# Routed experts with four places for transposed rows, TensorE products without a reader between stages, and an earlier compare in the scans' check

## The chip, the cores and the metric

The kernel runs on one core of a Trainium2 chip. The metric is the device time of one execution in microseconds (us), as the median of several runs. The core has a matmul engine (PE in the profile; its weight loads have a row of their own, PEld), a vector engine (DVE), an activation engine (ACT), GpSimd (POOL), which here issues gathers, and SyncE (SP), which issues all other transfers. The engines meet by counting semaphores only.

## The reference

The input x has 2 sequences of 2048 tokens with 512 channels. Four layers follow one another, each added to x:

```python
x = x + cond_layer(x, cond)       # per channel: x times a gate worked out from cond
x = x + rnn(x)                    # h = tanh(x_t @ Wx + h @ Wh + b), from token to token
x = x + moe(x, cond)              # 2 shared experts, and the 2 best of 8 routed experts, per token
x = x + leaky(cond, x)            # g = sigmoid(h @ Wh.T + z_t @ Wz.T + b); h = tanh(h * (1 - alpha) + g * z_t)

def moe(x, t):
    shared = sum(silu(x @ w1[e].T) * (x @ w3[e].T) @ w2[e].T for e in (0, 1)) / 2
    s = sigmoid([x, t] @ W_router.T); best two by s + bias; gates = s_best / sum(s_best)
    routed = sum(gelu(x @ r1[e].T) @ r2[e].T * gate[e] for e in best two)
    return (shared + routed) / 4
```

## The kernel before

**Stages.** `build` runs five blocks one behind the other: the first scan (`rnn`), the shared experts for half of the tokens (`shared_part` 0, with the router in it), the routed experts (`routed_part`), the other half of the shared experts (`shared_part` 1, which also gathers what the routed experts wrote), and the second scan (`leaky`). A block ends with a barrier of all engines, so a stage starts when the last engine has come out of the one before.

**Scans.** A sequence is cut into 32 segments that are scanned side by side, 16 chunks of 4 steps. A warm round comes first, then one full round (`full_round`). At its last step (`is_end`) DVE takes the difference of the states at the segments' ends from those before (L572) and its largest value per partition (L573); PE turns that column into a row of `pm` (L353); DVE takes the row's largest (L655) and compares it with a tolerance (L656). The outcome, `running`, is read by every engine (`over_rounds`: each waits until `check` has reached 4 and loads the word), and with it each branches to another round or out of the block. DVE's last sum of a chunk (L588, x plus state) releases SP's store of that chunk (L198).

**Shared experts.** 64 items for each half. An item is 24 products of 512 columns into `p1` (L1062) and 12 into `p2` (L1077), in PE's order: first(n), then second(n - 1). Ahead of the first item ACT and DVE split the first weights and the first x into 16-bit parts (L1209, L1507; L1191, L1320). In part 0 PE waits ahead of it for `zeroed`, then for these splits. `px` is a bank of PSUM for the router's small products; `listed` tells that the list of tokens per expert (`token_of`) has been read out of it.

**Routed experts.** 71 tiles of 128 rows, each of one expert. For each tile t: POOL gathers 128 rows of both 16-bit parts into one of four places `rows` (L1722); SP transposes them by a DMA into `xt` (`turn_x`, L1731); PE makes 12 products of 512 columns into `pf` (`first`); ACT applies gelu (L1807) and casts (L1811), DVE makes the low part (L1825); SP transposes that result (`turn_h`, L1737) into `ht`; PE makes 12 products into `py` (`second`); ACT scales into `y` (L1801), SP stores it (L1741). PE's order is first(0), first(1), first(2), second(0), first(3), second(1), and so on. There are two places for `xt`. The transposes of tiles 0 and 1 are issued in the stage before. SP's list, in order, is

```python
for q in range(LEAD): load of 768 KB into stage[q][:, 0:TILE]      # L1744, two
for t in range(SLOT_TILES):
    turn_x(t + 2)      # waits for rows_in (the gather) and f_done >= t + 1
    turn_h(t)          # waits for hs_ready >= t + 1
    if t == 0: store_last(...)      # 1 MB, L1684
    if t >= 2: store(t - 2)
    if t == 2: load of 1 MB into xres     # L1757
```

SP does these one after the other, so a wait in one holds up all behind it. The gather of tile t waits until the transpose of tile t - 4 has landed.

## Time and profile before

| | us |
|---|---|
| median of 3 runs | 1998.11 |
| the runs | 1996.50, 1998.11, 1998.31 |
| the profiled execution, its own time | 1998.5 |
| its span, first to last instruction | 1996.6 |
| PE busy | 1954.5 (98%) |
| DVE, ACT, POOL busy | 1107.8, 804.3, 141.3 |
| mean granted clock of PE | 0.994 |

The profile page gives busy time, the chain that ended last and the costliest groups of instructions over the whole span. Each stage also shows in the timeline (instructions in order of time with the idle time before them and what ended it), in the table by windows (busy time of each engine, PE's granted clock and the DMA share in a stretch) and in the list of waits. A product's printed length in the timeline includes its way through the array: behind one another, products start closer together than they are long.

### The profile page before, as it was taken

Reading aid. Unit: us, or ns where it says so; the run is one execution under the profiler, and the core shown is the slowest. Engines: PE = TensorE matmul, PEld = TensorE weight load, DVE = VectorE, ACT = ScalarE, POOL = GpSimd, SP = SyncE. Lnnn points to the kernel's source line nnn. Section 1 sums busy time; section 2 is a strip of 40 time slices with the busy share of each in tenths; the row PEclk is TensorE's granted clock in tenths of the full one; section 3 lists DMA queues with packets and bytes.
Section 4 is the critical chain, followed back from the end, with each engine's and each line's share of the span. In section 5 each row is a group of like instructions: output and inputs, shape, how many; then the busy total and the mean of one; then the engine's idle time right before and its main releaser. Section 6 shows DMA issues by size and latency. Waiting matters only on the chain. (4 is left out here: it accounts for less than half of the span.)

```text
span 1996.6 us, 45523 instructions
## 1 busy us (share of the span) xinstructions
PE 1954.5 (98%) x18076; PEld 1180.6 (59%) x18076; DVE 1107.8 (55%) x2366; ACT 804.3 (40%) x1701; POOL 141.3 (7%) x144
## 2 busy tenths in 40 slices
PE   8999979999999999999999999999999999999997
PEld 6999944444444444444444444444455555999997
DVE  5666556544895654111111147555665664778887
ACT  4444445432121433343333345322332332566664
POOL 0000000000000000111111112111101110000000
PEclk9999989999999999999999999999999999999999
DMA  7033238654342533999999965433332352101111
GB/s 298 17 136 142 109 141 224 195 170 136 132 163 85 190 106 128 218 205 203 201 205 204 188 201 181 141 90 90 100 96 69 101 156 94 45 3 43 42 42 45
DMA packets 281903, 266.37 MB, mean 133 GB/s; under 512 B 225991, under 2 KB 233293, under 8 KB 275086
## 3 DMA queue, kind: packets, MB, share of 16 engines
q1 hardware_dynamic: 270942, 228.73, 39.9%
q0 software_dynamic: 10800, 35.40, 6.7%
q8 instruction: 113, 1.85, 0.4%
q14 instruction: 48, 0.39, 0.1%
HBM read 153.70 MB, written 56.36 MB: 105 GB/s over the span
## 5 line engine op out<-in xcount | busy, mean ns | idle before, releaser
L1062 PE MATMUL sh_p<-xh,arena 128*128 128x512 f16 x2048 | 611.2, 380 | 8.6 <-DVE xl L1320 6.3
L1062 PE MATMUL sh_p<-xl,arena 128*128 128x512 f16 x1024 | 389.1, 380 | 0.0
L1062 PEld LDWEIGHTS sh_p<-xh,arena 128*128 128x128 f16 x2048 | 200.6, 98 | 252.1 <-issue 10.4
L1077 PE MATMUL p<-sh_h_hi,arena 128*128 128x512 f16 x1024 | 304.6, 379 | 0.0
L1825 DVE SCALAR_TENSOR_TENSOR ro_hs<-ro_h,fac,ro_hs 128x512 f16<-128x512 f32 x71 | 53.4, 752 | 306.3 <-ACT ro_hs L1811 270.9
L1232 ACT CAST sh_h_hi<-sh_half_h 128x512 f16<-128x512 f32 x128 | 79.1, 618 | 349.4 <-DVE sh_half_h L1590 346.0
L1768 PE MATMUL ro_pf<-arena,xres 128*128 x852 | 198.7, 384 | 7.1 <-DMA xres<-xl 4.8
L1768 PE MATMUL ro_py<-arena,ro_ht 128*128 x852 | 195.3, 379 | 0.7 <-DMA ro_ht<-ro_hs 0.7
L1226 ACT ACTIVATE sh_sig<-sh_p,fac 128x512 f32<-128x512 f32 x128 | 87.8, 686 | 268.1 <-PE sh_p L1062 268.1
L1077 PE MATMUL p<-sh_h_lo,arena 128*128 128x512 f16 x512 | 194.0, 379 | 0.0
L1062 PEld LDWEIGHTS sh_p<-xl,arena 128*128 128x128 f16 x1024 | 100.5, 98 | 121.6 <-issue 1.4
L1587 DVE SCALAR_TENSOR_TENSOR sh_half_h<-sh_sig,sh_p 128x512 f32<-128x512 f32 x128 | 87.6, 685 | 146.0 <-ACT sh_sig L1226 145.9
L1077 PEld LDWEIGHTS p<-sh_h_hi,arena 128*128 128x128 f16 x1024 | 96.7, 98 | 109.7 <-issue 0.4
L1768 PEld LDWEIGHTS ro_pf<-arena,xres 128*128 128x128 f16 x852 | 84.2, 99 | 110.7 <-issue 13.1
L1590 DVE TENSOR_TENSOR sh_half_h<-sh_half_h,sh_p 128x512 f32<-128x512 f32 x128 | 88.0, 688 | 109.2 <-PE sh_p L1062 106.2
L1768 PEld LDWEIGHTS ro_py<-arena,ro_ht 128*128 128x128 f16 x852 | 83.3, 98 | 101.4 <-issue 1.2
L1594 DVE TENSOR_TENSOR sh_h_lo<-sh_half_h,sh_h_hi 128x512 f16<-128x512 f32 x128 | 88.6, 692 | 71.7 <-ACT sh_h_hi L1232 71.2
L283 PE MATMUL leaky_acc<-leaky_x_hi,leaky_wx_hi 128*128 128x256 f32 x368 | 112.0, 304 | 1.5 <-DVEq L536 0.4
L1807 ACT ACTIVATE ro_h<-ro_pf,fac 128x512 f32<-128x512 f32 x71 | 48.8, 687 | 146.4 <-PE ro_pf L1768 146.4
L283 PE MATMUL leaky_acc<-leaky_x_hi,leaky_wx_lo 128*128 128x256 f32 x368 | 103.7, 282 | 0.0
L283 PE MATMUL leaky_acc<-leaky_x_lo,leaky_wx_hi 128*128 128x256 f32 x368 | 103.5, 281 | 0.0
L283 PE MATMUL rnn_acc<-rnn_x_hi,rnn_wx_hi 128*128 128x256 f32 x336 | 98.7, 309 | 2.7 <-issue 2.6
(272 smaller groups left out, 3100.2 us busy)
## 6 DMA issues: line engine op xcount, KB each, us to landing
stage<-in_shared_w SPq DMA_DIRECT2D x29, 768.0 KB, 5.3
routed_rows<-xres SPq DMA_DIRECT2D x71, 256.0 KB
stage<-in_norms_r SPq DMA_DIRECT2D x16, 1024.0 KB, 4.9
stage<-in_routed_w SPq DMA_DIRECT2D x16, 1024.0 KB, 4.8
stage<-in_norms SPq DMA_DIRECT2D x14, 1024.0 KB, 5.1
arena<-x SPq DMA_DIRECT2D x12, 1024.0 KB, 5.8
rnn_xs<-in_x SPq DMA_DIRECT2D x8, 1024.0 KB, 18.8
x<-xres SPq DMA_DIRECT2D x16, 512.0 KB, 2.6
```

The source lines that it names most:

```text
L283: mm = nc.tensor.matmul(acc[p][:, m, :], w[:, k, cols], x[p][:, k, :], start=(not gate and m % 2 == 0 and k == 0 and x is x_hi and w is wx ...
L1062: mm = nc.tensor.matmul(p1[u % P1][:], arena[:, w:w + P], x[slot(gl)][:, :, k, :], start=(j == 0), stop=(j == 3 * KD - 1))
L1077: mm = nc.tensor.matmul(p2[m][:], arena[:, w:w + P], h[n % 2][:], start=(i == 0 and j == 0), stop=(i == HID - 1 and j == 2))
L1226: nc.scalar.activation(sig[n % 2][:], p1[2 * n % P1][:], ACT.Sigmoid, scale=fac[:, 0:1]).then_inc(sig_ready, 1)
L1232: nc.scalar.copy(h_hi[n % 2][:], full_h[n % 2][:]).then_inc(hh_ready, 1)
L1587: nc.vector.scalar_tensor_tensor(half_h[n % 2][:], sig[n % 2][:], 2.0 ** -41, p1[2 * n % P1][:], ALU.mult, ALU.mult).then_inc(p1_free, 1)
L1590: nc.vector.tensor_tensor(full_h[n % 2][:], half_h[n % 2][:], p1[(2 * n + 1) % P1][:], ALU.mult).then_inc(p1_free, 1)
L1594: nc.vector.tensor_tensor(h_lo[n % 2][:], full_h[n % 2][:], h_hi[n % 2][:], ALU.subtract).then_inc(h_ready, 1)
L1768: mm = nc.tensor.matmul(out, a[:, lhs + k * P:lhs + (k + 1) * P], experts[:, bass.ds(e, 1), w0 + w + k * D:w0 + w + (k + 1) * D].rearrange ...
L1807: nc.scalar.activation(h[t % 2], pf[t % 2][:], ACT.Gelu, scale=fac[:, 2:3]).then_inc(g_done, 1)
L1825: nc.vector.scalar_tensor_tensor(hs[t % 2][:, D:2 * D], h[t % 2], fac[:, 3:4], hs[t % 2][:, 0:D], ALU.mult, ALU.subtract).then_inc(hs_read ...
```

## The change

There are four edits.

1. First scan, end of the full round: PE gets seven products of 128x512 in front of its wait for the check's column and four behind the product L353. They write `pg[0]`, which nobody reads by then. Shared part 0 gets 20 products of 128x128 ahead of its wait for `zeroed`, and five of 128x512 at its end, behind a wait for `listed`; both write `px`.
2. Check, in both scans: DVE's wait for PE's row, the reduce (L655) and the compare (L656) move from the end of the round into the last step, ahead of the product with the decay (L581, second scan only), of the last sum (L588) and of the copy L653.
3. Routed experts: four places for `xt`; the two new ones are the last quarters of the two stage buffers, beside the part that the 768 KB loads fill.
4. SP issues turn_x(2) and turn_x(3) ahead of its loop, and in the loop turn_x(t + 4) in place of turn_x(t + 2), with the same value of f_done awaited. POOL's and PE's waits on `xt_in` go by four semaphores.

```diff
                     full_chunks(pe, r, chunk)
+                    if gate:
+                        idle_products(nc, pg[0][:], wr_hi[:, 0, 0:P], wr_hi[:, 1, :], 7)
                     pe.wait_ge(check, (r - 1) * CHECK_LINKS + 2)
                     nc.tensor.matmul(pm[0:1, 0:P], mx[:, 0:1], ident[:], start=True, stop=True).then_inc(check_row, 1)
+                    if gate:
+                        idle_products(nc, pg[0][:], wr_hi[:, 0, 0:P], wr_hi[:, 1, :], 4)
...
+                        if is_end(c, o) and j == CHUNK_STEPS - 1:
+                            dve.wait_ge(check_row, turn[0])
+                            tied(nc.vector.tensor_reduce(mx[0:1, 3:4], pm[0:1, 0:P], AX.X, ALU.max))
+                            tied(nc.vector.tensor_scalar(running[:], mx[0:1, 3:4], TOL, None, ALU.is_gt))
                         if leaky:
                             dve.wait_ge(hi_ready, (s + 2) * parts)
...
                     nc.vector.tensor_copy(e_prev[:], hist[1][:, :, CW - LANES:CW - BATCH])
-                    dve.wait_ge(check_row, r)
-                    tied(nc.vector.tensor_reduce(mx[0:1, 3:4], pm[0:1, 0:P], AX.X, ALU.max))
-                    tied(nc.vector.tensor_scalar(running[:], mx[0:1, 3:4], TOL, None, ALU.is_gt))
...
                 if first_part:
+                    idle_products(nc, px[:, 0:P], keep["ident16"][:], keep["ident16"][:], 20)
                     pe.wait_ge(zeroed, 1)
...
                 second(ITEMS - 1)
+                if first_part:
+                    pe.wait_ge(listed, 1)
+                    idle_products(nc, px[:], keep["ident16"][:], h_hi[0][:], 5)
...
+def idle_products(nc, out, w, x, count):
+
+    for _ in range(count):
+        nc.tensor.matmul(out, w, x, start=True, stop=True)
...
-    return [both[:, i * 2 * D:(i + 1) * 2 * D] for i in range(2)]
+    behind = [s[:, TILE:MATRIX].bitcast(F16) for s in keep["stage"]]
+    return [both[:, i * 2 * D:(i + 1) * 2 * D] for i in range(2)] + behind
...
-                    pool.wait_ge(xt_in[t % 2], 16 * ((t - RING) // 2 + 1))
+                    pool.wait_ge(xt_in[t % XT], 16 * ((t - RING) // XT + 1))
...
                     sp.wait_ge(rows_in[t % RING], 16 * (t // RING + 1))
-                    if t >= 2:
-                        sp.wait_ge(f_done, t - 1)
-                    sp.dma_start_transpose(xt[t % 2].rearrange("p (q n) -> p q n", n=P), rows[t % RING]).then_inc(xt_in[t % 2], 16)
+                    if t >= XT:
+                        sp.wait_ge(f_done, t - XT + 1)
+                    sp.dma_start_transpose(xt[t % XT].rearrange("p (q n) -> p q n", n=P), rows[t % RING]).then_inc(xt_in[t % XT], 16)
...
+                for t in range(2, XT):
+                    turn_x(t)
                 for t in range(SLOT_TILES):
-                    if t + 2 < SLOT_TILES:
-                        turn_x(t + 2)
+                    if t + XT < SLOT_TILES:
+                        turn_x(t + XT)
                     turn_h(t)
...
-                    pe.wait_ge(xt_in[t % 2], 16 * (t // 2 + 1))
+                    pe.wait_ge(xt_in[t % XT], 16 * (t // XT + 1))
                     if t >= 2:
                         pe.wait_ge(g_done, t - 1)
-                    product(pf[t % 2][:], xt[t % 2], e, 0).then_inc(f_done, 1)
+                    product(pf[t % 2][:], xt[t % XT], e, 0).then_inc(f_done, 1)
```

## Rows read from the trace of the kernel before

**Rows 1.** The page's first line.

```profile
span 1996.6 us, 45523 instructions
```

**Rows 2.** Timeline of PE, first scan to shared part 0: start us, length us, what.

```profile
262.93 0.65 PE L300 MATMUL rnn_acc<-rnn_h_lo,rnn_wr_hi 128*128 128x64 f16 x16
265.40 0.38 PE L353 MATMUL rnn_pm<-ident,rnn_mx 128*1 128x128 f32 x2 [1.83 <-DVE rnn_mx L573]
272.13 1.01 PE L1062 MATMUL sh_p<-xh,arena 128*128 128x512 f16 x2 [6.35 <-DVE xl L1320]
...
277.94 0.38 PE L1062 MATMUL sh_p<-xl,arena 128*128 128x512 f16 x1
```

**Rows 3.** Windows there: stretch, length, busy PE, PEld, DVE, ACT, POOL, clock, DMA.

```profile
267.50:268.00 0.50, 0.00 (x0) 0.00 (x0) 0.00 (x0) 0.00 (x0) 0.00 (x0) 0.59 0.99 393
```

**Rows 4.** Timelines of DVE and SP there, and one row of SP's waits (264 to 275).

```profile
266.25 0.27 DVE L655 TENSOR_REDUCE rnn_mx<-rnn_pm 1x1 f32<-1x128 f32 x1
266.56 0.14 DVE L656 TENSOR_SCALAR rnn_running<-rnn_mx 1x1 int32<-1x1 f32 x1
...
266.17 0.33 SPq L198 DMA_DIRECT2D x<-xres  x1
...
SPq L161 <- PEq L161: 1.6, 1, 1.6
```

**Rows 5.** Timeline of DVE and PE, shared part 0 to routed experts.

```profile
782.35 2.48 DVE L1308 SCALAR_TENSOR_TENSOR arena<-stage,scl,arena 128x1024 f16<-128x1024 f32 x2 [1.77 <-ACT arena L1186]
...
783.28 0.38 PE L1077 MATMUL p<-sh_h_lo,arena 128*128 128x512 f16 x1
786.02 7.04 PE L1768 MATMUL ro_pf<-arena,xres 128*128 x24 [2.36 <-PEq L895]
794.69 2.76 PE L1768 MATMUL ro_pf<-arena,xres 128*128 x12 [1.62 <-DMA xres<-xl]
797.28 2.75 PE L1768 MATMUL ro_py<-arena,ro_ht 128*128 x12
803.19 4.45 PE L1768 MATMUL ro_pf<-arena,xres 128*128 x12 [3.15 <-DMA xres<-xl]
807.48 2.75 PE L1768 MATMUL ro_py<-arena,ro_ht 128*128 x12
```

**Rows 6.** Windows of the routed experts: at the start, and from 808 us on.

```profile
786.00:786.50 0.50, 0.48 (x2) 0.29 (x3) 0.50 (x2) 0.40 (x1) 0.50 (x1) 0.91 1.59 184
...
808.00:1158.00 350.00, 350.00 (x1624) 158.62 (x1623) 54.11 (x72) 138.45 (x208) 59.07 (x62) 1.00 0.92 201
```

**Rows 7.** Timeline of SP's issues and of POOL's first gather there.

```profile
785.11 0.81 SPq L1744 DMA_DIRECT2D stage<-in_shared_w  x2
790.55 1.24 SPq L1731 DMA_TRANSPOSE xres<-xl  x1
792.76 1.23 SPq L1737 DMA_TRANSPOSE ro_ht<-ro_hs  x1
...
794.72 2.00 SPq L1731 DMA_TRANSPOSE xres<-xl  x1
796.77 2.47 SPq L1737 DMA_TRANSPOSE ro_ht<-ro_hs  x1
799.34 3.31 SPq L1731 DMA_TRANSPOSE xres<-xh  x1
...
785.75 0.94 POOL L1722 DMA_INDIRECT xh<-x_rows,token_of  x1 [125.78 <-POOLq L895]
```

**Rows 8.** DMAs that write or read xres, 780 to 840 us: issue to landing.

```profile
DMA to landing us min/median/max: 3.9/4.6/8.3
```

**Rows 9.** Timeline of DVE at the end of the second scan.

```profile
1990.05 0.49 DVE L578 TENSOR_TENSOR leaky_h_lo<-leaky_hist,stage 128x128 f16<-128x128 f32 x2
...
1990.80 0.42 DVE L588 TENSOR_TENSOR leaky_xo<-leaky_xs,leaky_hist 128x256 f32<-128x256 f32 x1
```

**Rows 10.** Windows behind the last compute: the last chunk's store.

```profile
1992.00:1993.00 1.00, 0.00 (x0) 0.00 (x0) 0.00 (x0) 0.00 (x0) 0.00 (x0) 0.50 0.94 385
```

5 lines of the change are left out of this document (3 added, 2 removed).

## The prediction

> **What bounds the kernel now.** I read the span first [rows 1] and PE's busy share in the table above it: 98%. So whatever the four edits can give back lies in the few microseconds in which PE stands still or runs at the lower clock. The timeline of PE around each barrier shows these, the windows show the granted clock, the timelines of SP and DVE show what comes last. In the middle of the routed stage there is nothing to win: from 808 to 1158 us PE is busy for all of 350 us at clock 1.00, with the DMA engines at 0.92 [rows 6].
>
> Every time below is in us of the profiled execution.
>
> *First scan to shared part 0.* The scan's last products end at 263.6, the check's product runs at 265.40, the first shared product at 272.13 [rows 2]. Between 267.5 and 268.0 the granted clock falls from 2.4 to 1.2 GHz (mean 0.59 in that half microsecond) [rows 3], some 4 us after the scan's last dense products. So the shared stage starts slow: from 272.13 to 277.94 it starts 14 products [rows 2], while at the full clock one takes 0.216 (2.59 for 12, the distance from 794.69 to 797.28 [rows 5]). 14 x 0.216 = 3.0, against 5.8: **2.8 us lost to the clock**.
>
> *Shared part 0 to routed.* PE ends at 783.6 and comes back at 786.02; DVE's last split ends at 784.83, so the barrier waits for DVE, not for PE [rows 5]. The clock falls inside 786.0 to 786.5 (mean 0.91) [rows 6], when PE is already back. The 24 products of tiles 0 and 1 take 7.04 as printed, less the 0.16 by which a printed group of twelve (2.75) outlasts its distance to the next (2.59): they hold PE until 792.9, where 24 x 0.216 = 5.2 would give 791.2, **1.7 lost**. Then PE waits for x of tile 2 until 794.69 (**1.8**), and from 799.9 for x of tile 3 until 803.19 (**3.3**); the clock falls again and first(3) takes 4.3 in place of 2.6 (**1.7**) [rows 5]. Together 8.5.
>
> *The end.* The last sum starts at 1990.80, and behind it only the last store and the way out follow: the store moves data in 1992 to 1993 [rows 9, 10], the span ends at 1996.6 [rows 1].
>
> **The change, part by part.**
>
> *Eleven products at the end of the first scan.* Seven take 7 x 0.216 = 1.5 and end near 264.9; the check's product waits for DVE until 265.40 anyway [rows 2], so they hide. They'd cost if they ran at the lower clock: 3.0, to 266.4, one late. The four behind it take 0.9, to about 266.7. PE's wait for the outcome is queued behind them, and the outcome came at 266.70 before [rows 4]. They cost nothing as long as it comes no earlier, and otherwise eat what the compare gives.
>
> *Twenty small products in shared part 0.* A quarter of the columns each: an estimate from 0.216 is 1.1 in all at the full clock and 2.1 at the lower. They start when the barrier opens, near 269.8 (SP's wait for PE there began 1.6 earlier, and PE was the last at it [rows 4]), and end at 270.9 or 271.9. PE isn't wanted before 272.13 [rows 2]; what hides them is the splitting of the first x. If that were 1 us shorter they would cost at the lower clock.
>
> *What the clock gives there.* No row shows a gap of this kind filled in part. Of the 8.5 us between 263.6 and 272.13, 3.5 or so get filled: two pauses remain, 3.1 (266.7 to 269.8) and 1.2. The lower bound is nothing: the 2.4 us pause before 786.02 sufficed to bring the clock down [rows 5, 6], and this one is longer. The upper bound is all 2.8, if the clock never falls. The 24 products at 786 got the clock back before they were done; at 272 it took 5.8 us of half-rate work. The nearest row for a partial gain is one of 1.7, what the shorter slow stretch at 786 lost. I take half of that, **-0.85**, as I can't tell whether it falls on the good side. The Trainium skill ("TensorE: Matmul & The Clock Gate", Part 1) says that the same kernel runs into the switch at different points in different runs. The runs of before lie 1.8 apart, which fits a switch of this size; by that rule the gain here would be 0 in some runs and 1.7 or 2.8 in others.
>
> *The compare moved up, first scan.* DVE's reduce and compare stood behind the last sum and the copy: 266.25 to 266.70 [rows 4]. Now they start when PE's row is there, near 265.9, and the outcome comes at about 266.3: up to 0.4 earlier for ACT and PE. The last sum starts 0.6 later, at 266.35, and so SP issues its store at 266.8 in place of 266.17; queued behind it are SP's own wait for the outcome and the barrier. SP had 1.6 of slack there, waiting for PE [rows 4], so this hides. Gain between 0 (the four products eat it) and 0.4: **-0.35** if PE's sequencer does not wait for its array; I take that.
>
> *The compare moved up, second scan.* Here nothing hides it. The two low parts end at 1990.54. Wait, reduce, compare (0.27 + 0.14 and the hops between them, as spaced in the first scan: 266.25 to 266.70) are 0.45 to 0.6 ahead of the product with the decay and the last sum. The last sum and with it the last store move from 1990.80 to about 1991.36: **+0.56**. What leaves from the other end (reduce and compare, to 1991.77) had lain beside the store's flight, so nothing is given back. Bounds 0.4 and 0.7 [rows 9, 10].
>
> *Five products at the end of shared part 0.* 1.1, from 783.5 to 784.6; `listed` had come long ago (the gathers of tiles 0 to 3 need it and are over), so the wait is free. DVE arrives at 784.83 [rows 5], so they hide. The pause shrinks from 2.4 to 1.3. If the clock holds, PE has tiles 0 and 1 done at 791.2.
>
> *Four places, and the order on SP.* The wait on f_done in the loop has the same value at the same turn, so the only new freedom at the start is that x of tiles 2 and 3 is issued right behind the two loads, near 786, and not at 790.55 and 794.72 [rows 7]. Before, x of tile 3 was queued behind the 1 MB store (L1684, between the issues at 792.76 and 794.72) and took 8.3 to land, where 4.1 (790.55 to 794.69) is what tile 2 took [rows 5, 7, 8]. But the DMA engines are at work on the loads' 1.5 MB until about 791 (1.57 MB at the 385 GB/s at which the last store of the program moves [rows 10] are 4.1 us, and I allow 1.8 from the issue at 785.11 [rows 7] to the first byte). I put x of tile 2 at 793.0 (bounds 790, 4.1 behind its new issue, and 794.7, as before), and x of tile 3 1.3 later.
>
> What is late next is h. On SP, turn_x(4) now stands ahead of turn_h(0). It waits for the gather of tile 4, issued at 785.75, which passes the same DMA engines as the loads [rows 7]; I put its landing at 792. Then turn_x(4) issues to 793.3, turn_h(0) to 794.5 (before: 792.76 to 793.99), and h(0) lands 4.1 behind its issue, at 797.5. Queued behind that: the 1 MB store, turn_x(5), turn_h(1), each as before with an x in front, 0.5 to 1 later than the 796.77 of before [rows 7]; one more gather shares the engines. With 7 to 8 us from its issue, as its neighbour x(3) had, h(1) lands at 804.5 to 805.6. PE's run is then: first(2) 793.0 to 795.6; second(0) 797.6 to 800.2; first(3), in place, to 802.8; second(1) from 805.1. Before, second(1) started at 807.48 [rows 5]: **-2.4**. From there h(2), behind turn_x(6), has 5 us of room, and so does h(3) behind the 1 MB load. So of 8.5 some 6 stay, as waits for h in place of waits for x. Bounds: 0.7, if the clock falls in the wait for h(1) and takes its 1.7 again, and 8.5.
>
> The Trainium skill ("DMA: Bandwidth & Descriptors", Anatomy of one DMA) says that the DMA engines never wait on a semaphore, the issuing sequencer does. That is the rule that speaks against this order: turn_h(0) can't pass a turn_x(4) that waits. The trace's spacing of SP's issues agrees.
>
> *Sum.* -0.85 - 0.35 - 2.4 + 0.56 = -3.0. The profiled execution took 1998.5 (span 1996.6 and 1.9 around it), 0.4 above the median. 1998.5 - 3.0 = 1995.5, and against the median 1998.1 - 3.0 = **1995.1**.
>
> **The rivals.**
>
> *A. The x transposes were the whole trouble.* h(0) and h(1) land in time, because the loads leave room and x no longer queues behind the store; both clock losses of the routed start go. For it: x of tile 3 alone lost 3.3 and 1.7 [rows 5]. Against: SP's order. Routed start -4.5 to -8.5, first boundary -1.7 to -2.8, compare +0.2: between -6 and -11, likeliest -6.1: 1992.0. The whole of it is 1987.0.
>
> *B. The queue ahead of h decides (slower).* Behind 1.5 MB of loads each transpose may take not 1.24 but 3.31 to issue, as the one at 799.34 did [rows 7]. Then x(2), x(3), x(4) are out at 785.9 + 9.9 = 795.8, h(0) at 799.1, the store takes 0.6, and x(5) and h(1) are out at 803.0 and 806.3, and with 8.3 from h(1)'s issue start at 803.0 to landing [rows 8] second(1) starts at 811.3, 3.8 later than before; one more fall of the clock makes it 5.5. With +0.56 - 0.35: 2002.1 to 2003.8. It decides from the point where turn_h(1) is issued more than 2.5 us later than at 796.77. Against: x(2) at 790.55 was issued in 1.24 while the loads were still moving.
>
> *C. The products and places do nothing that shows.* The clock falls as before (pauses of 3.1 and 1.3 are left) and h(1) comes when x(3) used to and PE waits as long: -0.7 in the routed stage, +0.2 in the checks: 1997.6.
>
> **How the numbers follow.** My forecast 0.50, with its own range 1993.4 (both clock terms whole) to 1996.9; A 0.25; C 0.18; B 0.07. A change of 0.2%, 4.0 us, is about the least that a measurement tells from none. Faster by more than that means below 1994.1: A nearly whole (0.23) and a third of the forecast's lower side (0.15): 0.38. Slower, above 2002.1: most of B, 0.05. The rest, 0.57, lies within. For 8 in 10 the range goes from 1990.5, which takes in most of A, to 1998.3, which takes in C.
>
> **What would show it.** In the trace after: the first shared product's clock and the distance of its first 14 products; the two windows at 267.5 and at 272 to 278; PE's first product of the routed stage some 1 to 3 earlier, its 24 products in 5.2; who releases first(2), second(0), first(3) and second(1): h in place of x if I'm right, none if A is; SP's turn_h(0) and turn_h(1) against 792.76 and 796.77; the last sum of the second scan 0.56 later behind its step's low parts. Wrong would make me: a gather of tile 4 that lands before 790, which puts turn_h(0) in front; loads whose share of the DMA engines delays x(2) beyond 795; or new code that shifts the way of an engine through the branch and the barriers, of which no row of before gives a price.

## The result, and the profile after

| | before | after |
|---|---|---|
| median, us | 1998.32 (10 runs, 1996.02 to 2000.51) | 2003.07 (10 runs, 2001.64 to 2011.41) |
| ratio to before, with its 95% interval | | 1.0033 (1.0025 to 1.0041) |
| the profiled execution, us | 1998.5 | 2001.64 |
| its span | 1996.6 | 1999.8 |
| PE busy | 1954.5 | 1957.7 |

The change makes the kernel slower by 4.8 us. I had forecast 3.0 us less. The profiled execution of after is the shortest of its ten, so the trace shows 3.2 us of the 4.8.

Where they lie: I go from boundary to boundary. The first line of the routed experts starts at the same time in both traces, so everything ahead of it evens out.

PE from the end of the first scan to shared part 0, timeline of the kernel after (start, length, what, idle before and who ended it):

```profile
263.82 1.67 PE L1684 MATMUL rnn_pg<-rnn_wr_hi 128*128 128x512 f16 x7
265.80 0.38 PE L355 MATMUL rnn_pm<-ident,rnn_mx 128*1 128x128 f32 x2 [0.32 <-DVE rnn_mx L577]
266.12 1.04 PE L1684 MATMUL rnn_pg<-rnn_wr_hi 128*128 128x512 f16 x4
271.61 2.24 PE L1684 MATMUL sh_px<-ident 128*128 128x128 f16 x20 [4.46 <-PEq L161]
273.91 1.01 PE L1067 MATMUL sh_p<-xh,arena 128*128 128x512 f16 x2
```

The windows of after in the same stretch (stretch, length, busy time of PE, PEld, DVE, ACT, POOL, granted clock, DMA share, GB/s):

```profile
267.50:268.00 0.50, 0.00 (x0) 0.00 (x0) 0.00 (x0) 0.00 (x0) 0.00 (x0) 1.00 0.02 8
271.00:272.00 1.00, 0.39 (x5) 0.42 (x6) 0.00 (x0) 0.41 (x1) 0.00 (x0) 0.86 0.11 25
272.00:273.00 1.00, 1.00 (x12) 1.00 (x10) 0.65 (x1) 1.00 (x3) 0.20 (x1) 0.50 0.63 70
275.00:276.00 1.00, 1.00 (x5) 0.39 (x4) 1.00 (x3) 1.00 (x3) 0.00 (x0) 0.94 1.00 410
```

At 267.5, where before fell to the lower level [rows 3], the clock of after is still at 2.4 GHz. It falls at the end of 271 and is back early in 275, so only the small products and the first few real ones run slow. But PE comes out of the barrier at 271.6 and meets its first real product at 273.91, 1.8 later than before [rows 2]. The clock's gain and this delay cancel: the 24 products of the routed experts start at 786.01, before at 786.02 [rows 5].

PE at the start of the routed experts, timeline of after:

```profile
783.50 1.24 PE L1684 MATMUL sh_px<-sh_h_hi,ident 128*128 128x512 f16 x5
786.01 5.35 PE L1788 MATMUL ro_pf<-arena,xres 128*128 x24 [1.27 <-PEq L900]
797.54 4.34 PE L1788 MATMUL ro_pf<-arena,stage 128*128 x12 [6.18 <-DMA stage<-xl]
802.07 2.76 PE L1788 MATMUL ro_py<-arena,ro_ht 128*128 x12 [0.18 <-DMA ro_ht<-ro_hs]
...
809.04 2.76 PE L1788 MATMUL ro_py<-arena,ro_ht 128*128 x12 [1.62 <-DMA ro_ht<-ro_hs]
...
820.79 2.76 PE L1788 MATMUL ro_py<-arena,ro_ht 128*128 x12 [1.22 <-DMA ro_ht<-ro_hs]
```

Here is the loss. PE is done with tiles 0 and 1 at 791.2, 1.7 earlier than before, and then waits 6.18 for x of tile 2, where before it waited 1.62 [rows 5]. first(2) starts 2.85 later, at 797.54, at the lower clock; second(1) starts at 809.04 against 807.48, and one more wait, for h of tile 3, follows at 820.79. In sum the trace of after is even with before at 786, 1.6 behind at second(1), 3.3 behind at the start of shared part 1 (1168.15 against 1164.81) and 3.2 behind at the end.

SP's issues in that stretch, timeline of after:

```profile
785.12 0.81 SPq L1762 DMA_DIRECT2D stage<-in_shared_w  x2
785.98 7.67 SPq L1749 DMA_TRANSPOSE stage<-xl  x2
796.00 1.23 SPq L1749 DMA_TRANSPOSE xres<-xh  x1
797.27 1.33 SPq L1755 DMA_TRANSPOSE ro_ht<-ro_hs  x1
...
802.50 3.13 SPq L1755 DMA_TRANSPOSE ro_ht<-ro_hs  x1
```

x of tile 2 is issued at 785.98 in place of 790.55 [rows 7], 4.6 earlier, and lands later: 11.6 from issue to first(2), where before took 4.1. The two transposes take SP 7.67 to issue. Then SP stands still until 796.00, because turn_x(4) waits for the gather of tile 4 (f_done, its other wait, was up since about 789), and turn_h(0) is behind it, 4.5 later than before.

What the DMA engines did, windows of before and then of after:

```profile
791.00:793.00 2.00, 2.00 (x10) 0.74 (x8) 0.75 (x1) 0.92 (x2) 0.00 (x0) 1.00 1.27 241
795.00:797.00 2.00, 2.00 (x11) 0.89 (x10) 0.33 (x1) 0.00 (x0) 1.15 (x1) 1.00 1.08 380
```

```profile
789.00:791.00 2.00, 2.00 (x11) 0.88 (x9) 0.71 (x1) 1.22 (x2) 0.00 (x0) 1.00 1.00 351
791.00:793.00 2.00, 0.36 (x2) 0.00 (x0) 0.16 (x2) 1.41 (x2) 0.00 (x0) 1.00 1.26 104
793.00:795.00 2.00, 0.00 (x0) 0.00 (x0) 0.63 (x1) 0.00 (x0) 0.00 (x0) 0.74 0.91 199
795.00:797.00 2.00, 0.00 (x0) 0.00 (x0) 0.00 (x0) 0.00 (x0) 0.00 (x0) 0.50 1.35 132
```

Up to 791 the loads stream as before. From 791 to 797 the DMA engines of after are busy (share 1.26, 0.91, 1.35) and move only 104 to 199 GB/s; before moved 241, 170 and 380 in the same three windows. What PE waits for isn't idle, it is slow. The queues' rows tell whose packets were slow. Queue q0 has the gathers, q1 all that SP issued. From 790 to 792, packets, MB and share of the 16 engines' time of q0, before and then after:

```profile
q0 software_dynamic: 144, 0.49, 61.2%
q0 software_dynamic: 37, 0.14, 94.5%
```

In before 144 packets of the two gathers start in these 2 us, and x of tile 2 is issued only at 790.55. In after, where its transpose is already queued, 37 start, and they take more of the engines' time than the 144 did. From 792 to 794 only 16 are left in before, which then has 991 packets in q1; after still has 41 in q0 and 176 in q1.

The end of the second scan, timeline of after:

```profile
1992.61 0.49 DVE L582 TENSOR_TENSOR leaky_h_lo<-leaky_hist,stage 128x128 f16<-128x128 f32 x2
...
1994.09 0.42 DVE L596 TENSOR_TENSOR leaky_xo<-leaky_xs,leaky_hist 128x256 f32<-128x256 f32 x1
```

From the low parts to the last sum it is 1.48, before 0.75 [rows 9]: 0.73 more.

### The profile page after: what moved, and what is told of

Its sections match the earlier page's. It is cut to its first block and busy times, and to the rows that moved or that the text cites. A ratio compares the mean times of both kernels' runs of the same rounds, so it can differ in the third digit from the quotient of the medians.

```text
span 1999.8 us, 45594 instructions
## 1 busy us (share of the span) xinstructions
PE 1957.7 (98%) x18112; PEld 1183.3 (59%) x18112; DVE 1108.1 (55%) x2366; ACT 804.6 (40%) x1701; POOL 141.8 (7%) x144
## 5 line engine op out<-in xcount | busy, mean ns | idle before, releaser
L1788 PE MATMUL ro_pf<-arena,stage 128*128 x420 | 97.9, 384 | 6.2 <-DMA stage<-xl 6.2
L1788 PE MATMUL ro_pf<-arena,xres 128*128 x432 | 99.0, 379 | 1.3 <-PEq L900 1.3
```

What stands on the lines that cost most here:

```text
L1788: mm = nc.tensor.matmul(out, a[:, lhs + k * P:lhs + (k + 1) * P], experts[:, bass.ds(e, 1), w0 + w + k * D:w0 + w + (k + 1) * D].rearrange ...
```

## The experiments

Sixteen kernels ran, each in several rounds beside the kernel before; the ratio is to the runs of before on the same chip. The last three columns are from each kernel's one trace: the time from PE's first routed product to first(2), to second(1), and to the first product of shared part 1 (the whole stage). They can be compared across kernels whatever happened ahead of the routed stage.

| kernel | median, us | before | ratio (95%) | to first(2) | to second(1) | whole stage |
|---|---|---|---|---|---|---|
| before | | | | 8.7 | 21.5 | 378.8 |
| after | 2003.07 | 1998.32 | 1.0033 (1.0025, 1.0041) | 11.5 | 23.0 | 382.1 |
| e1 edits 3 and 4 | 2004.76 | 1998.27 | 1.0041 (1.0026, 1.0056) | 11.5 | 24.6 | 382.6 |
| e2 edit 1 | 1996.54 | 1998.27 | 0.9992 (0.9983, 1.0000) | 8.7 | 18.2 | 376.2 |
| e3 edit 2 | 1998.87 | 1998.27 | 1.0004 (0.9995, 1.0012) | 8.7 | 21.2 | 378.5 |
| e4 e1, loads late | 1999.63 | 1998.27 | 1.0008 (0.9999, 1.0017) | 5.2 | 18.6 | 378.7 |
| e5 four places, SP's old list | 2001.52 | 1997.83 | 1.0018 (1.0009, 1.0027) | 11.5 | 21.7 | 383.1 |
| e6 e1, h ahead of x | 2006.28 | 1997.83 | 1.0045 (1.0031, 1.0059) | 11.1 | 23.9 | 386.0 |
| e7 before, loads late | 1999.61 | 1997.83 | 1.0006 (0.9997, 1.0015) | 6.4 | 17.6 | 375.6 |
| e8 the five products | 1998.33 | 1997.83 | 1.0005 (0.9996, 1.0014) | 8.3 | 18.8 | 376.2 |
| e9 e1, transposes ahead of the loads | 2001.60 | 1998.15 | 1.0022 (1.0013, 1.0031) | 5.2 | 22.3 | 380.1 |
| e10 e1, gathers held | 2003.44 | 1998.15 | 1.0026 (1.0016, 1.0036) | 7.1 | 24.7 | 382.4 |
| e11 before, 1 MB store and load late | 1996.52 | 1998.15 | 0.9994 (0.9985, 1.0003) | 8.5 | 18.0 | 377.3 |
| e12 e11 with edit 1 | 1997.92 | 1998.15 | 1.0003 (0.9994, 1.0012) | 8.8 | 18.3 | 377.5 |
| e13 e1, gathers early | 1999.94 | 1998.14 | 1.0009 (1.0000, 1.0018) | 7.2 | 21.2 | 378.9 |
| e14 before, gathers early | 1998.56 | 1998.14 | 0.9997 (0.9988, 1.0005) | 7.0 | 20.0 | 377.3 |
| e15 two places, edit 1, gathers early, 1 MB store and load late | 1995.15 | 1998.14 | 0.9982 (0.9973, 0.9990) | 7.7 | 17.1 | 376.2 |
| e16 as e15 with edits 3 and 4, 768 KB loads at the end | 1994.22 | 1998.14 | 0.9983 (0.9972, 0.9993) | 5.2 | 17.1 | 375.5 |

The time to first(2) repeats well: 8.3 to 8.8 in the six kernels in which x of tile 2 waits for first(0) and follows the loads (before, e2, e3, e8, e11, e12), 11.1 to 11.5 in the four (after, e1, e5, e6) in which it is issued right behind the loads with the gathers under way. The four kernels with the routed code of before fall in two pairs: before and e3, whose first 24 products ran partly at the lower clock, have 21.5 and 21.2 to second(1) and 378.8 and 378.5 for the stage, e2 and e8, whose 24 ran at 2.4 GHz, 18.2 and 18.8, and 376.2 both. So these columns are read only beside the medians. Five traces are of executions well below their kernel's median, by 3.3 to 4.4 us (e4, e6, e7, e9, e13); what the longer executions of these kernels lost, and where, no trace shows.

The explanations in play after the result were four: SP's order (h behind an x that waits), the loads ahead of the transposes, the gathers beside them, and the products that delay the way through the first barrier. The expectations give them letters; each says what its letters stand for.

**Which edit.** First each edit alone.

e1, the places and SP's list alone (edits 3 and 4 of the diff, whole functions `turned_x` and `routed_part`, and the four `xt_in`).

> The kernel before with edits 3 and 4 alone: four places for xt, and SP's list with turn_x(2) and turn_x(3) ahead of its loop and turn_x(t + 4) in it. Theory Q (the queue): in the changed kernel the two transposes behind the 1.5 MB of loads took 7.67 us to issue, x of tile 2 let PE wait until 797.54, and turn_h(0) came 4.5 us later than before; PE reached second(3) 2.95 us later although its clock had held. Alone, with the clock lost at the start as before, this gives 3 to 6 us over the kernel before, and most of the 4.8 that the changed kernel is over it in the medians. Rival P (the products and the longer way out of the first scan cost the time): alone, these two edits are within 1.5 us of the kernel before.

6.5 us slower than before, a little beyond the 3 to 6 of theory Q and far from rival P. Its trace repeats that of after (24 products in 5.35, 6.12 of waiting for x of tile 2, turn_h(0) at 798.15), 1.1 later, without any of the idle products.

e2, the idle products alone (edit 1).

> The kernel before with edit 1 alone, all 36 products without a reader. Theory Q: they give back clock: 1.7 us at the start of the routed stage, up to 2.6 at the start of shared part 0, against up to 1.5 for a later barrier (the changed kernel's PE came out of the first scan's branch 4.9 us behind the compare, before 3.1): the time is 1 to 3 us under the kernel before. Rival P: the products hold PE up on its way through the branch and the barrier and cost more than the clock gives: 1 to 4 us over.

1.7 faster, interval 0 to 3.4.

e3, the compare alone (edit 2).

> The kernel before with edit 2 alone, the compare ahead of the last sums in both scans. Theory Q: +0.7 us in the second scan (the trace of the changed kernel has 3.29 of distance from the low parts to the end where before it was 2.57 at the step before), 0 to -0.4 in the first: +0.3 to +0.7, not to be told from none. Rival: the later store of the first scan holds the barrier: +1.0 or more.

0.6 slower, not told apart from none; the 0.73 of the trace of after lies in the interval. The three medians add up to 6.5 - 1.7 + 0.6 = +5.4, where all together measured +4.8. The loss is in the routed edits.

**SP's order.** e6 is e1 with the loop turned round:

```diff
-                    if t + XT < SLOT_TILES:
-                        turn_x(t + XT)
                     turn_h(t)
+                    if t + XT < SLOT_TILES:
+                        turn_x(t + XT)
```

> Edits 3 and 4 alone, with turn_h(t) ahead of turn_x(t + 4) in SP's loop. Theory L in its first form (turn_x(4) holds turn_h(0) up until the gather of tile 4 has come): h(0) is issued near 791 in place of 797, PE waits for it no more, 2 to 4 us under the 6.5 that the list with x ahead costs: 2000 to 2002. Rival M (the two transposes behind the loads are the cost): h(0) is queued behind their 7.5 us of issuing all the same, x of tile 2 lands near 797: within 1.5 us of the kernel with edits 3 and 4.

SP and PE in e6, timeline:

```profile
784.32 7.23 SPq L1734 DMA_TRANSPOSE stage<-xl  x2
791.59 3.38 SPq L1740 DMA_TRANSPOSE ro_ht<-ro_hs  x1
...
795.42 5.30 PE L1773 MATMUL ro_pf<-arena,stage 128*128 x12 [5.71 <-DMA stage<-xl]
```

turn_h(0) gets out 7.2 behind PE's first product, in e1 11.0 (798.15 against 787.12), and nothing is won: 8.5 slower than before. PE still waits 5.7 for x of tile 2. That turn_x(4) stands ahead of turn_h(0) is not the cause.

e5 keeps SP's list of before, with four places (the diff is against e1):

```diff
-                for t in range(2, XT):
-                    turn_x(t)
                 for t in range(SLOT_TILES):
-                    if t + XT < SLOT_TILES:
-                        turn_x(t + XT)
+                    if t + 2 < SLOT_TILES:
+                        turn_x(t + 2)
```

> Four places for xt, but SP's list as before: no transpose ahead of the loop, turn_x(t + 2) in it. Only x of tile 2 comes earlier (it no longer waits for f_done), right behind the loads; x of tile 3 stays behind h(0) and the 1 MB store. The kernel with edits 3 and 4 alone was 6.5 us over the kernel before. Theory L (the list, two x in a row and x(t + 4) ahead of h(t)): this kernel loses most of that, 0 to 2.5 us over the kernel before. Rival M (any transpose behind the 1.5 MB of loads, beside the gathers, is slow): x of tile 2 lands near 797 and PE waits for it as long: 4 us over or more.

The difference to before is that every turn_x waits for two tiles less: turn_x(2) not for first(0), turn_x(5) for first(1) and not for first(3), and so on. The trace of e5:

```profile
785.92 0.81 SPq L1747 DMA_DIRECT2D stage<-in_shared_w  x2
786.78 2.29 SPq L1734 DMA_TRANSPOSE stage<-xl  x1
...
798.28 5.20 PE L1771 MATMUL ro_pf<-arena,stage 128*128 x12 [6.12 <-DMA stage<-xl]
...
808.09 0.40 SPq L1760 DMA_DIRECT2D xres<-x  x1
808.59 1.42 SPq L1734 DMA_TRANSPOSE xres<-xh  x1
...
817.98 2.76 PE L1771 MATMUL ro_pf<-arena,xres 128*128 x12 [1.56 <-DMA xres<-xh]
```

Against PE's first product x of tile 2 is issued 4.5 earlier than before (786.78 with 786.80, before 790.55 with 786.02), and it comes 11.5 after that issue, not 4.1. The kernel loses 3.7, more than theory L allowed and a little less than rival M. But that one transpose isn't where its trace loses them. x of tile 3 is there by then, so first(3) runs without the wait of 3.15 that before has, and second(1) starts 21.7 behind PE's first product, before 21.5. The stage's other 4.1 come later, most of them in two more waits for x: 1.56 for tile 5 at 817.98 and 1.92 for tile 7 at 830.43. Tile 5 shows the same thing once more. Before held turn_x(5) back until first(3) was done, 3.0 us behind the 1 MB load (807.72 against 804.72), and it landed 5.3 later (813.06); e5 issues it 0.5 behind that load, and it lands 9.4 later.

**The loads.** e4 is e1 with the two 768 KB loads at turns 12 and 14:

```diff
-                for q in range(LEAD):
-                    sp.dma_start(keep["stage"][q][:, 0:TILE], src["shared_w"][q + 1]).then_inc(stage_in, 16)
...
                     turn_h(t)
+                    if t in (12, 14):
+                        q = (t - 12) // 2
+                        sp.dma_start(keep["stage"][q][:, 0:TILE], src["shared_w"][q + 1]).then_inc(stage_in, 16)
```

> Edits 3 and 4 alone, and SP's two loads of 768 KB moved from the start of the routed stage to the turns of tiles 12 and 14, where nothing waits for them soon. Theory Q: with no loads in front, the two early transposes issue in 1.24 us each and land some 4 us later, near 790; PE has x of tile 2 in time, h(0) lands by 795, and the routed stage begins 5 us or more faster than in the kernel before: 1990 to 1995. Rival H (SP's order is what costs, turn_x(4) waiting for the gather in front of turn_h(0)): the gathers still come when they come, and the gain against the kernel before is under 2 us.

Timeline of e4, SP, POOL and PE:

```profile
783.16 2.61 SPq L1734 DMA_TRANSPOSE stage<-xl  x2
787.25 0.94 POOL L1725 DMA_INDIRECT xl<-x_rows,token_of  x1 [1.27 <-DMA stage<-xl]
...
795.21 4.04 PE L1774 MATMUL ro_py<-arena,ro_ht 128*128 x12 [3.23 <-DMA ro_ht<-ro_hs]
```

POOL's gather of tile 6 starts when x of tile 2 has landed: 787.25, 4.1 behind its issue. Two transposes are issued in 2.61, not in 7.24 as in e1. PE runs through tile 2 without a stop and then waits for h(0). Of the 6.5 us, 5.1 come back. Theory Q had put the kernel at 1990 to 1995, below before, and that was missed: by its median e4 is no faster than before, as rival H had it, since waits for h take the place of those for x (3.23 here, 2.03 at 815.24).

e7 is the same move in the kernel before.

> The kernel before with one thing changed: SP's two loads of 768 KB are issued at the turns of tiles 12 and 14, not at the start of the routed stage. It tells what the loads themselves cost. If the loads are what x of tile 2 and the gathers wait for, PE's 1.8 us wait for x(2) and part of the 3.3 for x(3) go: 2 to 5 us under the kernel before. If the order of x, h and the store decides, x(2), issued when f_done is 1, lands as before and the time is within 1 us.

1.8 slower, no clear difference, and neither of the two outcomes expected. In its trace first(2) comes 2.3 earlier, PE still waits 3.25 for x of tile 3, behind the 1 MB store, and the whole stage is 3.2 shorter than before's; but this execution lies 4.0 below the kernel's median, and what the others lose no trace shows. In the medians, then, late loads give nothing to the kernel before and 5.1 to the one with early transposes: the gain of e4 is not a plain gain of loads out of the way.

e9 is e1 with the two transposes ahead of the two loads.

```diff
+                for t in range(2, XT):
+                    turn_x(t)
                 for q in range(LEAD):
                     sp.dma_start(keep["stage"][q][:, 0:TILE], src["shared_w"][q + 1]).then_inc(stage_in, 16)
-                for t in range(2, XT):
-                    turn_x(t)
```

> Edits 3 and 4 alone (6.5 us over the kernel before), with the two early transposes issued ahead of the two loads and not behind them. Theory M (transposes behind loads in flight are what is slow: 11.5 us from issue to landing in two traces, 4.1 without the loads): x of tiles 2 and 3 land some 4 us behind their issue, PE has no wait for x, and the kernel is 3 us or more under the one with edits 3 and 4, though waits for h stay: -2 to +3 against the kernel before. Rival G (it is the gathers of tiles 4 and 5, in flight at the same time, that the transposes hinder and wait for): no better than 1.5 us under the 6.5.

Timeline of e9:

```profile
783.70 2.61 SPq L1734 DMA_TRANSPOSE stage<-xl  x2
786.36 1.48 SPq L1749 DMA_DIRECT2D stage<-in_shared_w  x2
788.44 4.12 SPq L1734 DMA_TRANSPOSE xres<-xh  x1
792.61 4.39 SPq L1740 DMA_TRANSPOSE ro_ht<-ro_hs  x1
...
799.14 5.19 PE L1773 MATMUL ro_py<-arena,ro_ht 128*128 x12 [6.62 <-DMA ro_ht<-ro_hs]
```

first(2) runs at once, and the wait has moved on to the transposes that now stand behind the loads: x(4) takes 4.12 to issue, h(0) 4.39, and PE waits 6.62 for h(0). Three of the 6.5 come back. Whatever transpose follows the loads pays. The Trainium skill ("DMA: Bandwidth & Descriptors", Queues, rings and completion order) says that each DMA engine takes the descriptors of one ring in their order; e1 and e9, which differ in that order alone, agree with it (11.5 behind the loads, 4.1 ahead of them). The two new places in the stage buffers aren't slow in themselves: x of tile 2 goes to the same place in e1 and in e9.

**The gathers.** In e10 POOL issues the gathers of tiles 4 and 5 only when x of tile 3 has landed:

```diff
+                pool.wait_ge(xt_in[3], 16)
                 for t in range(RING, SLOT_TILES):
```

> Edits 3 and 4 alone, and POOL holds its first gathers of the routed stage (tiles 4 and 5) until x of tile 3 has landed, so that loads and the two early transposes have the DMA engines to themselves. Rival G: the transposes land by 794, as soon as the 1.5 MB are through (4.1 us), in place of 797.5. Theory M: they take as long, near 797. In either case the gathers, and with them turn_x(4) and turn_h(0) behind it, come later, so the time may be over the 6.5 us; the landing of x of tile 2, read from when PE starts first(2), is what tells.

Timeline of e10:

```profile
787.84 5.85 SPq L1735 DMA_TRANSPOSE stage<-xl  x2
...
794.95 2.76 PE L1774 MATMUL ro_pf<-arena,stage 128*128 x12
805.18 4.26 PE L1774 MATMUL ro_py<-arena,ro_ht 128*128 x12 [7.47 <-DMA ro_ht<-ro_hs]
```

The loads are ahead as in e1, but x of tile 2 is there within 7.1 of its issue. That is between the two forecasts, nearer to rival G's. So the loads alone go with some 3 of the 7.4 above 4.1, and the rest needs the gathers beside them. The kernel doesn't gain (+5.3), since the held gather now holds turn_x(4) and h(0) behind it.

e13 takes the gathers out of the way without holding anything: POOL issues them in the stage before, once the transposes of tiles 0 and 1 have landed.

```diff
+                    for t in range(ROWS_RING, ROWS_RING + 2):
+                        pool.wait_ge(keep["xt_in"][t - ROWS_RING], 16)
+                        nc.gpsimd.indirect_dma_start(row_ring(keep, t), None, dram["xt"], bass.IndirectOffsetOnAxis(ap=token_of[:, t:t + 1], axis=0)
+                                                     ).then_inc(keep["rows_in"][t % ROWS_RING], 16)
...
-                for t in range(RING, SLOT_TILES):
+                for t in range(RING + 2, SLOT_TILES):
```

> Edits 3 and 4 alone, with POOL's gathers of tiles 4 and 5 issued at the end of shared part 0, as soon as the transposes of tiles 0 and 1 have landed, and not at the start of the routed stage. Theory G (loads, transposes and gathers in flight together are what is slow): x of tiles 2 and 3 land within 3 us of the loads' end, turn_x(4) waits for no gather, turn_h(0) is issued by 794, and the time is 0 to 3 us over the kernel before in place of 6.5. Rival M (transposes behind loads alone are slow): first(2) starts 11 us behind the issue as before, 5 us over or more.

Timeline of e13:

```profile
784.88 5.84 SPq L1738 DMA_TRANSPOSE stage<-xl  x2
...
792.12 1.34 SPq L1744 DMA_TRANSPOSE ro_ht<-ro_hs  x1
...
792.08 2.76 PE L1777 MATMUL ro_pf<-arena,stage 128*128 x12 [1.83 <-DMA stage<-xl]
```

7.2 from issue to first(2) again, turn_x(4) right behind the others (at 790.83), h(0) at 792.12. 1.8 slower than before: 4.7 of the 6.5 us are back, with the loads where they were, as theory G had it. e14, the same move in the kernel before, does nothing:

> The kernel before with the same two gathers issued in the stage before. Theory G: x(2), issued at 790.55 into the gathers' data, lands a little sooner; x(3), behind the 1 MB store, does not: 0 to 2 us under the kernel before. Rival M: no difference, within 0.5.

+0.4 in the medians, and PE's two waits for x are 1.62 and 3.36, much as before. So in the medians the early gathers are worth something only where the transposes are early.

Set side by side, from the SP and PE timelines of each trace, where PE waited for x of tile 2 (in e10 it was there by first(2) at the latest):

| | x(2) issued after the loads' issue | issue to use | loads' issue to use |
|---|---|---|---|
| gathers under way: after, e1, e5, e6 | 0.9 | 11.1 to 11.6 | 12.0 to 12.4 |
| gathers under way: e2, e8, e11, e12 | 3.7 | 5.9, 5.5, 5.7, 6.0 | 9.6, 9.2, 9.4, 9.7 |
| gathers under way: before, e3 | 5.4, 5.3 | 4.1, 4.3 | 9.6, 9.6 |
| gathers elsewhere: e10, e13 | 0.9 | 7.1, 7.2 | 8.0, 8.1 |
| gathers elsewhere: e14, e15 | 3.7 | 4.1, 4.8 | 7.9, 8.6 |

With the transposes ahead of the loads or the loads away it is 4.1 (e4, e9) or 3.5 (e7) from issue to landing with the gathers under way and 5.1 without (e16). Read down the last column: behind the loads, x of tile 2 comes 7.9 to 8.6 after their issue, whenever it was issued itself, as long as no gather is beside them. With the gathers it comes at 9.2 to 9.7 if it is issued 3.7 or more behind the loads, and at 12.0 to 12.4 if it is issued at once. In these rows an earlier issue wins nothing, and beside the gathers the earliest one loses some 3.

**The products.** e8 has only the five products at the end of shared part 0.

> The kernel before with only the five products at the end of shared part 0. All 36 products together gave 1.7 us. If the clock at the start of the routed stage is what they give back, this alone gives it: PE's first 24 products in 5.3 and not 7.0, but x of tile 2 lands when it did, so the 1.7 turn into a longer wait for x and the time stays within 0.5 us. The other theory, that the gain reaches the end: 1 to 1.7 us under.

Timeline of e8, SP and PE:

```profile
788.26 0.81 SPq L1753 DMA_DIRECT2D stage<-in_shared_w  x2
791.98 1.24 SPq L1740 DMA_TRANSPOSE xres<-xl  x1
...
789.14 5.35 PE L1777 MATMUL ro_pf<-arena,xres 128*128 x24 [1.25 <-PEq L895]
797.48 4.03 PE L1777 MATMUL ro_pf<-arena,xres 128*128 x12 [2.99 <-DMA xres<-xl]
```

The 24 products are fast, and up to first(2) what they gain becomes a longer wait for x: 2.99, where before it was 1.62. The table above has the reason: x is issued 1.7 earlier behind the loads (3.7, not 5.4) and comes hardly earlier (9.2, not 9.6). Behind it the trace does better than before: the wait for x of tile 3 is 0.84 and not 3.15, and the whole stage is 2.6 shorter. The medians still show no gain (+0.5, interval from 0.8 faster to 2.8 slower). The two fit together if the executions of before mostly have a stage as short as e8's and its trace shows one of the longer, which a single trace can't show. And the 5.35 isn't the products' doing alone: of the twelve kernels without these five, nine have it too (e1, e4, e5, e6, e7, e9, e11, e13, e14), and three have 6.90 to 7.04 (before, e3, e10). All six with them have 5.35.

**Store and load of 1 MB.** e11 is before with store_last at turn 4 in place of 0 and the 1 MB load at turn 6 in place of 2, e12 the same with edit 1.

```diff
-                    if t == 0:
+                    if t == 4:
                         store_last(sp, keep, 0, x_out)
...
-                    if t == 2:
+                    if t == 6:
```

> The kernel before with the 1 MB store issued at the turn of tile 4 and the 1 MB load at the turn of tile 6, in place of 0 and 2. x of tile 3 was queued behind that store and took 8.3 us to land, and PE waited 3.3 us for it and lost 1.7 to the clock behind the wait. Theory L2 (the store in front of x(3) is the cost): x(3) lands 4 to 5 us behind its issue, before PE wants it, and the time is 3 to 5 us under the kernel before. Rival: the waits move to tiles 5 to 7, within 1 us.

1.6 faster, interval from 3.0 faster to 0.6 slower, less than the 3 to 5 of theory L2. The wait for x of tile 3 is gone (turn_x(3) is issued at 793.83 in 1.26), that for x of tile 2 is not (3.19).

> The kernel before with edit 1 (all products) and the store and load of e11. If both gains are real and independent, -1.7 and -3 to -5: 4 to 7 us under the kernel before. If the store's place gives nothing: -1.7.

No difference. The two gains, -1.7 and -1.6, neither of them clear of none by itself, didn't add here; beside e11, edit 1 gave nothing.

**Together.** e15 joins what did no harm in the kernel with two places; e16 adds the four places, with the 768 KB loads at turns 66 and 67.

> Two places for xt as before, with all products of edit 1, the 1 MB store and load at tiles 4 and 6, and the two gathers in the stage before. Single gains measured: 1.7 for the products, 1.6 for the store's place, neither beyond its interval. If they add up with the gathers': 3 to 5 us under the kernel before. If each only fills the gap that another leaves, as the products with the late store did (0.2 under): 0 to 2.

3.0 faster than before (0.9982, 0.9973 to 0.9990).

> Edits 1, 3 and 4 with everything that collided taken apart: the two gathers in the stage before, the two 768 KB loads at the turns of tiles 66 and 67, the 1 MB store and load at tiles 4 and 6. Theory G: PE has no wait at the start of the routed stage beyond 1 us and its clock holds: 6 to 9 us under the kernel before, 1989 to 1992. Rival T (four places let SP and POOL run transposes and gathers ahead of h, in a stage whose DMA engines are 0.92 busy, whatever the start looks like): waits for h stay, and it is no more than 3 us under.

3.9 faster by the medians, 0.9983 (0.9972 to 0.9993) by the ratio, where theory G had hoped for 6 to 9. PE of e16, timeline:

```profile
785.99 5.35 PE L1791 MATMUL ro_pf<-arena,xres 128*128 x24 [1.26 <-PEq L899]
791.18 2.75 PE L1791 MATMUL ro_pf<-arena,stage 128*128 x12
796.25 4.45 PE L1791 MATMUL ro_py<-arena,ro_ht 128*128 x12 [2.32 <-DMA ro_ht<-ro_hs]
```

One wait is left at the start, for h as rival T had it, and the clock falls in it. Both kernels beat before and after, and they aren't told from one another. e16 differs from e15 in the four places and in the late 768 KB loads together, so what these runs show is that the pair brings nothing measurable over two places; four places alone, with the gathers early and the loads where they were, weren't tried against e15.

## Why the prediction was wrong

**The step that failed: "I put x of tile 2 at 793.0 (bounds 790, 4.1 behind its new issue, and 794.7, as before)".** It came at 797.5. The upper bound rested on the thought that an earlier issue can't land later. It can: in before, the wait for first(0) held the transpose back until the loads were nearly through, the gathers' packets went ahead of its own, and it then took 4.1; issued right behind the loads, with the gathers beside it, it takes 11.1 to 11.6. I had priced that wait as a cost, and it was one that did good. The first half of the sum was right, though no row had the 1.8 that I allowed from the loads' issue to their first byte: in the trace bytes move by 786.1, some 1.0 behind it, the loads stream until 791, and the two land 6.6 behind their issue, near 792. I then added the 2 us that were left of a transpose in free air, where the trace shows six more at 104 to 199 GB/s. By the trace of after, first(2) came 4.5 later than forecast and second(1) 3.9 later, so that the term of -2.4 measured +1.6. Another 1.8 is lost between second(1) and the end of the stage, where I had put nothing: I gave h(3), behind the 1 MB load, 5 us of room, and PE waits 1.22 for it at 820.79. It was issued at 812.63 and took 8.2 to its use. By the medians four places with the new list cost 6.5 (e1), four places with the old one 3.7 (e5).

**"What is late next is h": right, and too small.** turn_x(4) did wait for the gather of tile 4, with turn_h(0) behind it. I put that gather's landing at 792; turn_x(4) was issued at 796.00. h(0) was to land at 797.5 and was used at 802.07, h(1) at 809.04 in place of 804.5 to 805.6. But that order isn't what costs: with h in front (e6) the time is no better. The rule that I had weighed against the change (a sequencer's wait holds up what is behind it) is seen in SP's standing still from 793.65 to 796.00, and it wasn't the one that decided.

**Rival B had the mechanism.** Transposes behind 1.5 MB of loads were to take 3.31 each to issue, and from turn_h(1) more than 2.5 us late on it was to decide; the first two took 7.67 and turn_h(1) came 5.7 late (802.50 against 796.77). Its total was 2002.1 to 2003.8, and the median is 2003.07. I gave it 0.07, on the ground that x(2) "was issued in 1.24 while the loads were still moving". At 790.55 they were nearly through: the row showed the end of the queue, not its middle. The rows at 796.77 to 799.34 (2.47, 3.31) [rows 7], issued behind 1 MB in flight, were the nearer ones. B's path to the loss was not exact either: it had PE late from h(1) on, with second(1) 3.8 to 5.5 later than before, and the trace shows it late from x(2) on and second(1) 1.6 later. That its total fits the median is in part luck. Nor did B name the gathers, without which 4.7 of the 6.5 come back (e13).

**The clock at the first boundary: -0.85, of the right size as far as the traces tell.** The mean granted clock from 262 to 286 us is 0.93, 0.86, 0.86, 0.93 and 0.93 in the five kernels with edit 1 (after, e2, e12, e15, e16), and 0.79 in eight, 0.86 in five of the thirteen without the products of the scan. From the first shared product to the first routed one PE takes 511.7 to 512.9 in those five and 512.4 to 513.9 in the thirteen, 0.7 less in the mean, and the trace of before has the 513.9: so its 2.8 lost to the clock is likely more than most executions lose. In whole times the gain isn't shown. e2 is 1.7 faster, with an interval that reaches 0, and e12, which is e11 with edit 1, is 1.4 slower than e11, within their intervals. The Trainium skill ("TensorE: Matmul & The Clock Gate", Part 1), by which the same work meets the switch at different points in different runs, agrees with these rows, and with the 24 products at 786, which took 5.35 or 7 in kernels that are alike up to there.

**The 1.7 lost at 786 was partly an accident of one trace.** I read 7.04 [rows 5] as what the kernel does. Nine of twelve kernels without the five products show 5.35. So for most executions there may have been little for the five products to give back, and no gain from them is measured (e8, +0.5).

**The barrier.** PE came out of the first one at 271.6, 1.8 later than before, though the compare ended at the same time (266.67 and 266.70). I had named this as a way to be wrong ("new code that shifts the way of an engine through the branch and the barriers"). The products aren't needed for it: ACT's wait for the barrier is 4.7 in before and 6.0 in after, but of the twelve other kernels whose scan has no added product seven have 6.3 to 6.8 (e1, e3, e5, e7, e8, e10, e14) and five 4.0 to 4.3 (e4, e6, e9, e11, e13). It varies by up to 2.8 us between traces of the same code, and the trace of before was one of the short ones. All five with the products have 6.0 to 6.6, which so few traces can't tell from chance. So the 786.01 against 786.02 is a coincidence of two traces. The twenty small products cost nothing, but only just: they end at 273.85, and the first part of x is split at about 273.9 (DVE's split starts at 273.02, and 0.90 lay between its start and PE's product in before).

**The compare: -0.35 and +0.56.** In the first scan the new place saves 0.44 (the column's maximum starts 0.41 later than in before, the outcome comes 0.03 earlier); in the second it costs 0.73, a little over my upper bound of 0.7. The medians of e3 can't resolve either.

**What stays open.** That loads and gathers together make the early transposes slow is shown; why they do is not. The queues' rows tell that from 790 to 792 the gathers' packets take six times as long each beside the queued transpose (94.5% of the time for 37, against 61.2% for 144), and not why. By the Trainium skill ("DMA: Bandwidth & Descriptors", Queues, rings and completion order) the increment that reports a transfer is written after all earlier writes of that DMA engine, across its queues; a gather in POOL's queue could so hold back a transpose in SP's, and no run here tests that. Open too: the wide scatter of the kernels with early transposes (2001 to 2011, before 1996 to 2002), of which each trace shows one case, and what the executions of e4, e6, e7, e9 and e13 lose that lie 3.3 to 4.4 us above the traced ones. The 0.8 us that the trace of after wins back between the start of shared part 1 (3.3 behind before) and the low parts of the last step (2.6 behind) is mostly a wait for `half_h` in shared part 1: it is 0.74 in before and in e1, 0.3 in e12, and missing in the other fifteen traces.

## What to carry to other kernels

Before taking away a wait, look at what the waiting transfer would have met had it started at once; a wait that lets larger transfers through first can be the better order, and an earlier issue can land later. When such a wait goes, look at every transfer that it held, not at the first alone (x of tile 5 in e5). Bound the cost of an earlier transfer from rows in which it ran in the same company (queued behind a load, beside a gather), not from the rows in which it ran alone. A clock loss or a way through a barrier that is seen in one trace is one draw: before it is counted as a gain, it should be seen in several traces of code that is alike.

## What the runs showed of the hardware

- The transpose of 128 rows takes 3.5 to 5.1 us from issue to landing ahead of the loads or with the loads moved away (e4, e7, e9, e16), 7.1 to 7.2 right behind 1.5 MB of loads (e10, e13), and 11.1 to 11.6 right behind them with two gathers beside it (after, e1, e5, e6).
- The gathers' packets take longer too beside a transpose that is already queued: from 790 to 792 us 37 packets took 94.5% of the 16 DMA engines' time in after, and 144 took 61.2% in before.
- Its issue holds SP for 1.23 to 1.3 us in quiet, and right behind loads for 2.29 (one, e5), 2.9 (two in 5.85, e10) or 3.8 (two in 7.67, after); one took 4.39 in e9.
- With eleven products of 512 columns at the start of the pause behind the first scan, the granted clock fell between 270.7 and 272.0 in the five traces with them, in the trace of before at 267.5. With the stage's own products since about 274 it was back at 274.8 to 275.4 in three of them (after, e15, e16) and at 277.5 to 277.8 in two (e2, e12).
- The way out of the scan's last barrier differs by up to 2.8 us between traces of kernels with the same code there (ACT's wait 4.0 to 6.8).
